# Layer-0 scores of the newest batch ahead of the output projection of the batch before, with a new order of SP's queue

## What is computed

```python
# layer 0, per batch (8 heads of 40)
hs     = _mha(x @ Wq, enc @ Wk, enc @ Wv)            # enc = ctx[:73]
ca_q1  = einsum('btc,th->bch', ca, Wq_ca)[:, indices, :]   # ca = ctx[73:]
ca_hs1 = _mha(ca_q1, x, x)
ca_hs2 = _mha(ca_hs1 @ Wq, ca @ Wk_ca, ca @ Wv_ca)
x1     = (hs + ca_hs2) @ Wout + b_out + x
# layer 1, per batch (20 heads of 16), over all 77 tokens
out    = _mha(x1 @ Wq, ctx @ Wk, ctx @ Wv) @ Wo + bo + x1
```

## Time and profile before

| | us |
|---|---|
| median of 3 runs (400.5 to 403.73) | 401.69 |
| the profiled execution | 401.35 |
| its span | 399.6 |
| PE busy | 338.0 (85%) |
| DVE busy | 195.3 (49%) |
| ACT busy | 161.3 (40%) |
| POOL busy | 114.1 (29%) |
| mean granted clock of PE | 0.897 |

### The profile page before, as it was taken

One profiled execution on the slowest core, in us unless ns is written; L12 is line 12 of the kernel. 1 busy time (PEld: TensorE's weight loads), 2 busy tenths in 40 slices (PEclk: granted clock), 3 DMA queues, 4 the chain that ended last, 5 costly groups with the idle time before them and its releaser, 6 DMA issues.

```text
span 399.6 us, 7714 instructions
## 1 busy us (share of the span) xinstructions
PE 338.0 (85%) x2988; PEld 261.3 (65%) x2988; DVE 195.3 (49%) x421; ACT 161.3 (40%) x343; POOL 114.1 (29%) x118
## 2 busy tenths in 40 slices
PE   4998869999899998999899899979996977967305
PEld 2777565787667776877686678758874854764205
DVE  5561135727716883485358527834692362271111
ACT  3540643164428423663446264526452615205000
POOL 5835220341035115411531252134111201211001
PEclk9996999999759998998999999988998986598756
DMA  8998837522753676766666766776585253131140
GB/s 246 294 341 246 213 98 235 102 68 95 228 121 103 165 239 155 130 178 212 152 140 201 206 151 130 225 169 146 115 257 136 77 115 125 28 60 65 37 112 39
DMA packets 53543, 61.51 MB, mean 154 GB/s; under 512 B 18164, under 2 KB 45268, under 8 KB 53508
## 3 DMA queue, kind: packets, MB, share of 16 engines
q1 hardware_dynamic: 53508, 61.03, 57.3%
HBM read 38.22 MB, written 22.40 MB: 152 GB/s over the span
## 4 chain that ended last, share of the span: by engine, by line
PE 37%; DMA 26%; SPq 12%; DVE 10%; ACT 9%; issue 5%; DVEq 0%; ACTq 0%
DMA den<-u 6%; DMA atu<-u_scratch 4%; DMA u_scratch<-u 4%; ACT prob L732 3%; SPq L339 3%; DVE negm L839 3%; PE bank L602 3%; DMA q_scratch<-q 3%; DMA denc<-uc 3%; PE bank L678 2%; PE bank L592 2%; PE bank L464 2%; PE bank L434 2%; PE bank L642 2%; DVE negmc L839 2%
## 5 line engine op out<-in xcount | busy, mean ns | idle before, releaser
L839 DVE TENSOR_REDUCE negm<-bank 128x5 f32<-128x385 f32 (+2 forms) x88 | 42.5, 552 | 14.3 <-PE bank L712 14.3
L732 ACT ACTIVATE prob<-bank 77x512 f32<-77x512 f32 (+1 forms) x96 | 41.1, 530 | 19.0 <-PE bank L509 18.9
L1069 POOL TENSOR_TENSOR at0lo<-atu,at0hi 120x512 fp32r<-120x512 f32 x8 | 10.1, 1266 | 96.3 <-ACT at0hi L722 96.3
L1063 POOL TENSOR_TENSOR at1lo<-atu,at1hi 128x512 fp32r<-128x512 f32 x8 | 10.2, 1269 | 92.9 <-DVE at1hi L905 92.9
L801 ACT ACTIVATE prob<-bank 73x512 f32<-73x512 f32 x32 | 16.3, 592 | 46.9 <-PE bank L660 46.9
L507 PE MATMUL bank<-q,kp 32*77 32x256 f32 x320 | 27.9, 431 | 6.1 <-ACT prob L732 3.8
L434 PE MATMUL bank<-at1hi,wo1hi 128*128 128x256 f32 (+1 forms) x48 | 16.0, 334 | 19.0 <-issue 18.0
L839 DVE TENSOR_REDUCE negmc<-bank 128x2 f32<-128x512 f32 x48 | 29.4, 681 | 3.0 <-PE bank L519 2.9
L722 ACT ACTIVATE q<-bank 120x512 fp32r<-120x512 f32 (+3 forms) x32 | 15.7, 490 | 29.7 <-PE bank L438 29.4
L990 DVE TENSOR_TENSOR u<-u,rb 128x1280 f32<-128x1280 f32 x8 | 15.2, 1899 | 24.6 <-DMA rb<-rec_scratch 24.6
L642 PE MATMUL bank<-at0hi,wo 120*128 120x256 f32 x48 | 18.0, 376 | 9.8 <-issue 9.8
(11 more groups left out here) (152 smaller groups left out, 871.5 us busy)
## 6 DMA issues: line engine op xcount, KB each, us to landing
q_scratch<-q SPq DMA_DIRECT2D x24, 360.0 KB, 5.3
q0s<-q_scratch SPq DMA_DIRECT2D x8, 960.0 KB
xkeys<-in_xkeys SPq DMA_DIRECT2D x8, 512.0 KB, 3.4
u_scratch<-u SPq DMA_DIRECT2D x8, 512.0 KB, 3.5
xt<-in_xt SPq DMA_DIRECT2D x8, 384.0 KB, 4.9
rb<-rec_scratch SPq DMA_DIRECT2D x16, 192.0 KB, 3.7
out_t<-x SPq DMA_DIRECT2D x8, 384.0 KB, 2.4
rb<-rec_scratch SPq DMA_DIRECT2D x32, 80.0 KB, 3.1
```

The costliest lines, as they stand in the source:

```text
L732: nc.scalar.activation(p1[:, h:h + n, :].rearrange("p h q -> p (h q)"), ps_of("SC1", j, d)[0:KEYS1, 0:n * SQ], ACT.Exp, scale=SCALE1)\
L839: return nc.vector.tensor_reduce(out=out, in_=in_, axis=AX, op=ALU.max, negate=True)
```

## The change

On PE, SC0 and CT of batch b go ahead of O of batch c, in the job list and in the code. On SP, the q stores come before rbc, the wo load goes behind the q0s load, xkeys moves from the end of the slot before to behind the maxima, and denc goes ahead of the layer-1 atu loads. On DVE, rec1 goes behind the six copies of O.

```diff
--- before.py
+++ after.py
@@ -84,12 +84,14 @@
             jobs(0, "K1", *range(6))
         if s2:
             jobs(c, "EX")
+        if s1:
+            jobs(b, "SC0", 0, 1, 2, 3)
+            jobs(b, "CT", *range(6))
+        if s2:
             jobs(c, "O", 0, 1, 2)
         if s4 and not s1:
             jobs(e, "OUT", 0, 1)
         if s1:
-            jobs(b, "SC0", 0, 1, 2, 3)
-            jobs(b, "CT", *range(6))
             jobs(b, "PV0", 0, 1)
         if s2:
             jobs(c, "Q1", 0, 1)
@@ -324,34 +326,35 @@
                 if s2:
                     sp.wait_ge(recc_ready, c + 1)
                     sp.dma_start(rc_d.rearrange("e n -> (e n)").rearrange("(p n) -> p n", p=128), recc[:, :]).then_inc(recc_st, 16)
-                    if c == 0:
-                        sp.wait_ge(v2w_st, 32)
-                    sp.dma_start(wo0[96:128, :, 2, :].bitcast(f32), v_d[c]).then_inc(v2w_in, 16)
+                    sp.wait_ge(u0_ready, c + 1)
+                    sp.dma_start(u0_d.rearrange("o r j q -> (o r) j q"), u0[:, :, :]).then_inc(u0_st, 16)
+                if s1:
+                    drained(sp, "Q", b, 0, 1)
+                    for v, part in enumerate((q0hi, q0lo, q0hi)):
+                        sp.dma_start(q_d[:, :, v].rearrange("g r q -> r g q"), part.bitcast(f32)).then_inc(q_st, 16)
+                if s2:
                     sp.wait_ge(recc_st, 16 * (c + 1))
                     for odd in range(2):
                         sp.dma_start(rbc[64 * odd:64 * odd + 48, :, :].rearrange("p a c -> p (a c)"),
                                      rc_d[odd].unsqueeze(0).to_broadcast([48, PAIRS * CAD])).then_inc(rbc_in, 16)
-                    sp.wait_ge(u0_ready, c + 1)
-                    sp.dma_start(u0_d.rearrange("o r j q -> (o r) j q"), u0[:, :, :]).then_inc(u0_st, 16)
-                if s1:
-                    drained(sp, "Q", b, 0, 1)
-                    for v, part in enumerate((q0hi, q0lo, q0hi)):
-                        sp.dma_start(q_d[:, :, v].rearrange("g r q -> r g q"), part.bitcast(f32)).then_inc(q_st, 16)
-                if i == 0:
-                    sp.wait_ge(dve_init, 1)
-                    sp.wait_ge(k_st, 48)
-                    load_k0s(0)
-                if s2:
                     sp.wait_ge(u0_st, 16 * (c + 1))
                     if s4:
                         sp.wait_ge(at1lo_ready, e + 1)
                     for odd in range(2):
                         sp.dma_start(atu[0:120, odd, :], u0_d[odd, 0:D0, 0:3, :]).then_inc(at0u_in, 16)
                     sp.dma_start(atu[0:80, 2, :], u0_d[:, 0:D0, 3, :].rearrange("o r q -> r o q")).then_inc(at0u_in, 16)
+                if i == 0:
+                    sp.wait_ge(dve_init, 1)
+                    sp.wait_ge(k_st, 48)
+                    load_k0s(0)
                 if s1:
                     sp.wait_ge(q_st, 48 * (b + 1))
                     sp.dma_start(q0s[0:120, :, :].bitcast(f32), q_d.rearrange("g r v q -> (g r) v q")[0:H].rearrange("(h d) v q -> (d v) h q", d=D0))\
                         .then_inc(q0s_in, 16)
+                if s2:
+                    if c == 0:
+                        sp.wait_ge(v2w_st, 32)
+                    sp.dma_start(wo0[96:128, :, 2, :].bitcast(f32), v_d[c]).then_inc(v2w_in, 16)
                 def place_maxima():
                     drained(sp, "M0", b, 0)
                     sp.dma_start(q0s[120:121, :, :].bitcast(f32), mt0[:, :].bitcast(f32)).then_inc(q0s_in, 16)
@@ -363,6 +366,8 @@
 
                 if s1:
                     place_maxima()
+                    if b:
+                        load_xkeys(b)
                 if s3:
                     drained(sp, "PV1", d, 0, 1, 2)
                     sp.dma_start(den1[:, :], u1[D1:128:32, :, :]).then_inc(den1_in, 16)
@@ -398,6 +403,9 @@
                     for odd in range(2):
                         sp.dma_start(rb[64 * odd:64 * odd + 48, 0:4, :].rearrange("p a q -> p (a q)"),
                                      r0_d[odd].unsqueeze(0).to_broadcast([48, 4 * SQ])).then_inc(rb0_in, 16)
+                if s1:
+                    drained(sp, "CU", b, 0, 1)
+                    sp.dma_start(denc[:, :], uc[D0:128:64, :, :]).then_inc(denc_in, 16)
                 if s3:
                     sp.wait_ge(u1_st, 64 * (d + 1))
                     rows = u1_d.rearrange("j d s q -> (j d s) q")
@@ -406,11 +414,6 @@
                         sp.dma_start(atu[64 * odd:64 * odd + 64, 2, :], rows[256:320]).then_inc(at1u_in, 16)
                 if s4 and not s1:
                     store_out()
-                if s1:
-                    drained(sp, "CU", b, 0, 1)
-                    sp.dma_start(denc[:, :], uc[D0:128:64, :, :]).then_inc(denc_in, 16)
-                    if b + 1 < B:
-                        load_xkeys(b + 1)
             sp.wait_ge(out_st, 16 * B)
 
 
@@ -629,6 +632,22 @@
                         last = mm(ps[0:HT, 0:SQ], p2[:, half * HEADS0:(half + 1) * HEADS0, :].rearrange("p h t -> p (h t)"),
                                   expand[:, half, :], start=half == 0, stop=half == 1)
                     last.then_inc(full_of("EX", 0, c), 1)
+                if s1:
+                    pe.wait_ge(q0s_in, 32 * (b + 1))
+                    pe.wait_ge(k0s_in[b % 2], 16 * (b // 2 + 1))
+                    for j in range(4):
+                        ps = use("SC0", j, b)
+                        for e in range(2):
+                            h = 2 * j + e
+                            last = mm(ps[0:KEYS0, e * SQ:(e + 1) * SQ], k0s[b % 2][0:121, h, :], q0s[:, h, :], start=True, stop=True)
+                        last.then_inc(full_of("SC0", j, b), 1)
+                    pe.wait_ge(mtc_in, 16 * (b + 1))
+                    for k in range(3):
+                        for q in range(QT):
+                            ps = use("CT", 2 * k + q, b)
+                            mm(ps[:, :], gst[:, q * 128:(q + 1) * 128], cast[:, k * 512:(k + 1) * 512], start=True, stop=True)\
+                                .then_inc(full_of("CT", 2 * k + q, b), 1)
+                if s2:
                     if c == 0:
                         pe.wait_ge(whi_ready, 4)
                         pe.wait_ge(wlo_ready, 4)
@@ -651,20 +670,6 @@
                 if s4 and not s1:
                     output_projection()
                 if s1:
-                    pe.wait_ge(q0s_in, 32 * (b + 1))
-                    pe.wait_ge(k0s_in[b % 2], 16 * (b // 2 + 1))
-                    for j in range(4):
-                        ps = use("SC0", j, b)
-                        for e in range(2):
-                            h = 2 * j + e
-                            last = mm(ps[0:KEYS0, e * SQ:(e + 1) * SQ], k0s[b % 2][0:121, h, :], q0s[:, h, :], start=True, stop=True)
-                        last.then_inc(full_of("SC0", j, b), 1)
-                    pe.wait_ge(mtc_in, 16 * (b + 1))
-                    for k in range(3):
-                        for q in range(QT):
-                            ps = use("CT", 2 * k + q, b)
-                            mm(ps[:, :], gst[:, q * 128:(q + 1) * 128], cast[:, k * 512:(k + 1) * 512], start=True, stop=True)\
-                                .then_inc(full_of("CT", 2 * k + q, b), 1)
                     for k in range(2):
                         drained(pe, "SC0", b, 2 * k, 2 * k + 1)
                         if b == k == 0:
@@ -973,9 +978,6 @@
                     dve.wait_ge(ex_hi, c + 1)
                     tt(at0lo[96:128, 2, :], ps_of("EX", 0, c)[0:HT, 0:SQ], at0hi[96:128, 2, :].bitcast(f32), ALU.subtract)\
                         .then_inc(free_of("EX", 0, c), 1)
-                if s3:
-                    dve.wait_ge(den1_in, 16 * (d + 1))
-                    nc.vector.reciprocal(rec1[:, :], den1[:, :]).then_inc(rec1_ready, 1)
                 if s2:
                     if c >= 3:
                         dve.wait_ge(out_st, 16 * (c - 2))
@@ -983,6 +985,9 @@
                         is_full(dve, "O", m, c)
                         tt(x1[c % 3][:, m, :], ps_of("O", m, c)[:, 0:SQ], xt[c % 2][:, m, :], ALU.add)
                         tt(x1hi[:, m, :], ps_of("O", m, c)[:, 0:SQ], xt[c % 2][:, m, :], ALU.add).then_inc(free_of("O", m, c), 1)
+                if s3:
+                    dve.wait_ge(den1_in, 16 * (d + 1))
+                    nc.vector.reciprocal(rec1[:, :], den1[:, :]).then_inc(rec1_ready, 1)
                 if s4 and not s1:
                     layer1_out()
                 if s3:
```

8 lines of the change are left out of this document (4 added, 4 removed).

## The result

The changed kernel takes 458.58 us (median of 4 runs, 455.26 to 463.94) against 402.71 us of the kernel before in the same measurement (400.5 to 406.53): the ratio is 1.138 [1.126, 1.151], slower, by 56 us where I forecast 26 and bounded it at 41. A ratio leaves out executions over 1.5% above the fastest of their kernel, a median does not.

The account below looks back on a forecast made before the run. PE was taken as the bound, at 38.35 us a slot. Slots 2 to 6 lose 4.1 us each (20.5), slot 7 1.8, slots 1 and 8 4.1: 26.4 us on 401.35 gives 427.7 us, range 407 to 443.

Parts of the forecast that it names:

- X: The moment when DVE starts to copy O out; forecast to move from T + 25.8 to T + 27.5.
- T: Start of a slot, where PE takes up its batch's Q product; the next one forecast at X + 14.3, against 12.6.
- Step 1: SC0 on PE waits for the q0s stack, issued at T + 14.2 and taking 7.5 us; starts at T + 21.6.
- my own sign of being wrong: SC0 starting straight behind EX on PE, which would mean the stack loads quicker than slot 4 says.
- Step 2: O on PE runs at full clock without a gap, X 5.9 us after SC0's start: 1.7 us later than before.
- Step 3: Behind X, late rec1 delays xt and uc, so SM1's second half waits: 1.7 us lost, five times.
- Step 4: Lower PE clock behind the new idle time in SM1: 0.7 us, five times, bounds 0 and 2.6 us.
- Step 5: Remaining moves: rbc behind the q stores costed at nothing, hsc near T + 15.5; slots 1 and 8 together 4.1 us.
- clock and hsc: Rival: the new gap costs 2.6 us of clock each time and M0 comes 1 us late; near 442, chance 0.10.

Follow-up runs that it names:

- a1: The changed kernel with rbc issued ahead of the q stores again; 447.32 us, ratio 1.117.
- a3: The changed kernel with rbc ahead of the q stores and rec1 ahead of the copies again; 438.15 us, ratio 1.095.
- b3: The kernel before with only PE's new order, SC0 and CT ahead of O; 438.86 us, ratio 1.086.
- b1: The kernel before with only rbc moved behind the q stores; 435.34 us, ratio 1.088.
- b4: The kernel before with SP's new queue alone, PE and rec1 as before; 425.20 us, ratio 1.043.
- e3: The kernel before with SP's new queue but rbc ahead of q, and q stored twice, not three times; 407.14 us, ratio 1.013.

## Why the prediction was right and where it failed

Means over slots 2 to 7 of the changed kernel: X = T + 32.1 and next T = X + 14.5. Forecast: T + 27.5 and X + 14.3. Before: 25.8 and 12.6.

- **Step 1, start of SC0.** The stack left at T + 14.9 in the mean (forecast T + 14.2), but SC0 waited for it only in slots 0 and 7, since PE came late. SC0 starting straight behind EX was my own sign of being wrong. It came, in slots 1 to 6, but not because the stack was quick. The wait I described is real where PE isn't held earlier: a1, a3 and b3 show it in every full slot. SC0 starts there at T + 23.4 in the mean of a3 rather than T + 21.6, half of it because the stack leaves 0.9 us later (T + 15.1), half because the load takes 8.3 us (7.5 to 8.9 over the slots of the three). The one slot I had read it from gave 7.5. The estimate of 4.3 us came from a fit that the Trainium skill (DMA: Bandwidth & Descriptors, section Anatomy of one DMA — SWDGE (gpsimd) path) gives for DMAs issued by GpSimd. SP issues this one, and these times show that the fit doesn't carry over to it.
- **Step 2, O.** Right: no gap before it, full clock, 3.4 us. From SC0's start to X it was 6.6 us in slot 5, forecast 5.9; SC0 and CT still ran at the lower clock (0.59).
- **Step 3, the tail behind X.** Right in each link: rec1 at X + 2.0, xt issued at X + 5.7, PE held inside SM1 for uc. xt landed in 3.5 us instead of 4.9, so the half started at X + 10.6, not 11.9 (slot 5).
- **Step 4, the clock.** I took 0.7 us in this place. In slot 5 half of SM1 and the second CU took 4.4 us (288.09 to the next T, 292.53) against 2.4 in the forecast, 2.0 us more. This undersizing and step 3's early xt cancel by luck: slot 5 has X + 15.1, the forecast with its 0.7 us for the clock X + 15.0.
- **Step 5, "the rest", is the step that failed.** "rbc now stands behind the q stores and lands about when they do ... so I cost it at nothing." hsc ended at T + 16.7 in the mean (17.3 in slot 5), forecast T + 15.5. Worse, I compared M0's results with the stack, and never hsc with PE's arrival at S2, T + 14.1 in slot 5: even my own T + 15.5 made PE wait 1.4 us. Slot by slot it waits 1.5 to 5.1 us, and then comes what I left out altogether, the lower clock from S2 to EX, 4.6 us in slot 5. Over the six slots S2 starts 2.8 us later than before, and from S2 to X it takes 3.4 us more. b1 measures the term alone at 33 us. The rival "clock and hsc" named the late hsc, at 1 us a slot, but looked for the lower clock behind SM1 and not behind S2.
- **Sum.** The forecast for a slot was +4.1 us; it was +8.2: 6.3 ahead of X (forecast 1.7) and 1.9 behind it (forecast 2.4 with the clock). Six slots make 49 of the 62 us of the span. Slot 1 adds 6.9 where I had 1.3: it has the same wait of DVE for rbc (5.2 us), and PE waits 3.4 us for DVE behind it. Slot 1 also starts 4.6 us later, which I had not forecast; with SP's new queue or without it, its start varied from 53.3 to 61.0 us from kernel to kernel, and what sets it was not pursued.
- **Direction.** "Slower" was right, the reason only in part. Of the two waits for DMAs that were to take the place of one, the changed kernel shows the second (uc, behind rec1 and xt). The first, for the stack, is hidden behind the wait for rbc and comes out when that is taken back (a1). The range ended at 443 because its upper bound held rbc at zero.

What stays open is why rbc's issue takes 1.03 us instead of 0.38 behind the q stores (that the queue is full of their packets is argued from the order alone), why b4 costs less than b1, and why e3 is slower than e1 by more than wo's wait.

## What to carry over

When a small DMA is moved behind a large one on the same queue, cost its landing, not its issue, and set it against the moment when the first engine behind it runs out of work; here DVE already stood idle for it five times in the trace of before, and PE's cover was 1.4 to 3.4 us, against the 4.8 us by which hsc became later in the mean. Prices of moves that each hold up the same engine do not add: undoing one shows the next, so test each alone and each taken back. If a transfer is what is waited for, look first for bytes to leave out: here a third fewer stored gave more than any of the orders tried.

## What was not expected of the hardware

- The price of a gap in clock did not follow its length. Behind the gap of 2.9 us at S2, the jobs up to EX ran at 0.50 for 9.7 us (b1, slot 4), with 21.0 us more busy time over the program. Gaps of 3.4 to 6.1 us ahead of SC0 and CT cost 8.5 us of busy time (b3), though the rise in idle time was nearly three times as large. That it depends on which jobs follow (small ones at S2, wide ones at SC0) fits both, but no run varies it alone.
- 6 KB on ACT's own queue took 5.7 us beside the 960 KB load in flight, 2.2 us ahead of it; 96 KB behind that load took 7.9 us instead of 3.0.
- POOL's split of 64 x 256 took 1.86 us instead of 0.74 while DVE multiplied two SBUF tensors. The other way round, a multiply of 1.49 us took 4.01 beside a POOL instruction that began 0.1 us before it.
